# Starting eight expert units while the last routing is still being worked out

## The chip, the cores and the metric

The kernel runs on one core of a Trainium2 chip. Times are device microseconds of one execution; a profiled execution gives the trace. TensorE (PE) multiplies, VectorE (DVE) and ScalarE (ACT) work element by element, GpSimd (POOL) issues the DMAs that scatter rows to addresses read from a table, SyncE (SP) issues the others. The engines run their own instruction streams and wait for each other on semaphores.

## The reference

x has 3125 nodes of 256 values, and there are 50000 edges. Two GraphSAGE layers are followed by a mixture of experts:

```python
x = x + gnn(_layernorm(x), edge_index)              # two layers: mean over neighbours @ W_l + x @ W_r + b
x = x + moe(_layernorm(x))                          # _moe adds its tokens too: out = tokens + sum of experts
# _moe: softmax over 8 router scores, the two largest kept and scaled to sum 1
for e in range(E):
    h = jax.nn.gelu(tokens @ w1[e] + b1[e], approximate=False)
    y = h @ w2[e] + b2[e]
    out = out + combine[:, e:e + 1] * y
```

Only two experts of eight count for a node, so the kernel computes 6250 node-expert pairs.

## The kernel before

The nodes are 25 tiles of 128 (NT). The first 290 us build a matrix of edge counts and the first layer; that part is not touched. The stage in question begins at about 297 us.

**Sums.** For tile t TensorE adds 25 products (`aggregate`, L1306) into one of four PSUM buffers. VectorE reads them (`x2_and_var`), adds the residual and takes mean and variance; GpSimd raises the variance to -1/2 (`root`, L581); VectorE normalizes and writes the sum of both as the first content of `out` (`norm_and_sum`). TensorE turns and scores the tile two tiles later, between the products of `aggregate`.

**Routing.** Tiles go in 7 batches (`FIRST_OF` = 0, 4, 8, 12, 16, 20, 23). Per batch VectorE picks each node's two experts (`choose`), TensorE counts how many earlier nodes chose each expert (`prefix`), and VectorE turns that into row numbers (`place`). GpSimd then scatters each tile's normalized rows twice (`scatter`, L593, an indirect DMA of 128 rows), so that in `xs_dram` every expert has its rows one behind the other, in the order of the nodes. Behind the last batch VectorE lists the units: an expert's rows are cut into units of 256 (`PAIR`), the last of an expert filled up with padding. `tab_ri`, `tab_ei` and `tab_wi` hold a unit's first row, its expert, and, for every half of a unit, how many halves ahead of it must have been added to `out` before it may start.

**Units.** Then SP loads the rows of unit after unit (`load_rows`), TensorE turns them (`turn_rows`, L1439), multiplies by w1 (`hidden`, L1448) and by w2 (`result`, L1459); ScalarE copies and applies GELU (L1639, L1645); VectorE copies the expert's w1 (`keep_w1`, L1180), keeps each row's node and share (`keep_meta`) and adds b2 (`result`, L1175); ScalarE multiplies by the share (`weigh`, L1654). GpSimd adds the 128 rows of each half to their nodes in `out` with an indirect DMA that adds (L635). Four units of result rows have buffers (`ye`).

**Order of the additions.** Two halves may hold the same node, for two experts, and two such additions may not be in flight together. So GpSimd's stream is strictly in order, at most four additions are in flight, and each waits until as many ahead of it have landed as `tab_wi` says:

```python
pool.wait_ge(landed[q % NLAND], landed_before(n, q))
for d in range(1, NLAND):
    r = (q - d) % NLAND
    pool.wait_ge(landed[r], (before_it + (NLAND - 1 - r)) // NLAND * 16 + 32)
pool.wait_ge(S["ye_in"], n * HALVES + (q + 5))
```

The figure comes from counts per batch: for a half at place p, each expert's halves up to the end of batch b are counted as soon as the next expert's first half with nodes of that batch stands at p or ahead of it. The units run in rounds of four in a loop of 7 or 8 rounds; on these inputs there are 28 units, 56 halves and 7 rounds.

The first unit waits for the whole list, for all scatters and for all padding.

Of the kernel before, what the change touches and what calls it, by code (L numbers as in the profile page):

```python
# [5 lines left out]
F32 = mybir.dt.float32  # L6
# [8 lines left out]
P = 128  # L15
# [4 lines left out]
def build(nc, x, src, dst, w1l, w1r, b1, w2l, w2r, b2, router_w, ew1, eb1, ew2, eb2, out):  # L20
# [50 lines left out]
    FILLERS = 14  # L71
    XW = D + 8
    COEF, CHOSEN, NODE_ID = D, D + TOPK, D + 2 * TOPK
    assert NCH <= P and NCH * CHUNK == E and ALL_ROWS <= P and ALL_ROWS * ALL_COLS == E
    assert max(IN_BATCH) <= BATCH and FIRST_OF[-1] + BATCH <= NB * BATCH
    assert NW == NG * WPP and NW * WD == NT * P and NGROUP * GW == NW and NEED[-1] == NGROUP and KEYS <= P and GW == 2 * OF_BANK and OF_BANK % HALF == 0 and OF_BANK * P == 512

    with ExitStack() as ctx:
# [166 lines left out]
        end_i = later([NE], I32)  # L245
        assert oh_used[0] <= 2 * GW * (P + KEYS)

# [13 lines left out]
        def expert(shape, dt):  # L261
            n = 2
            for d in shape:
                n *= d
            if moe_used[0] % AC == 0:
                moe_used[0] += 2 * KD * D
            if moe_used[0] // AC != (moe_used[0] + n - 1) // AC:
                moe_used[0] = (moe_used[0] // AC + 1) * AC + 2 * KD * D
            assert moe_used[0] % AC + n <= AC
            return later(shape, dt, adj_flat, moe_used)  # L270
# [11 lines left out]
        hid_ps = [counts_ps[:, 2 + s, :] for s in range(2)]  # L282
# [19 lines left out]
        spread = adj[0:2 * NTAB, 2 * NE + 1, SPARE_AT - 4 * NTAB:SPARE_AT]  # L302
# [64 lines left out]
        def groups_of(t):  # L367
            return range(NEED[t + LEAD - 1], NEED[t + LEAD]) if t + LEAD < NT else range(0)

# [19 lines left out]
        def _(sp):  # L389
# [84 lines left out]
            with sp.Fori(FREE_TILES + NE, NT - 2) as t:  # L474
                node_tile(t)
            sp.wait_ge(S["zx_taken"], NT - 1)
            sp.dma_start(zi[:, :], z2_dram[(NT - 1) * P:, :]).then_inc(S["z_in"], 16)
            sp.dma_start(xt[0:LAST, :], x[(NT - 1) * P:N, :]).then_inc(S["x_in"], 16)
            sp.wait_ge(S["u_ready"], NT - 1)
            sp.dma_start(out[(NT - 2) * P:(NT - 1) * P, :], uo).then_inc(S["u_out"], 16)  # L480
            sp.wait_ge(S["u_ready"], NT)
            sp.dma_start(out[(NT - 1) * P:, :], uo[0:LAST, :]).then_inc(S["u_out"], 16)
            pad_experts(sp, range(0, NE // 2))
            for s in range(NLAND):
                sp.wait_ge(landed[s], 32)
            sp.wait_ge(S["table"], 1)

# [11 lines left out]
            load_rows(first_row, 0)  # L499
            load_rows(row_of(1), 1)  # L500
            third_row = row_of(2)
            sp.wait_ge(S["xe_tr"], 1)
            sp.wait_ge(S["meta_in"], 1)
            load_rows(third_row, 0)
            rounds = sp.value_load(nround_i[0:1, 0:1], min_val=MIN_ROUNDS, max_val=MAX_ROUNDS)

            with sp.Fori(0, rounds) as n:
# [15 lines left out]
        def _(pool):  # L523
# [59 lines left out]
            def scatter(t, j):  # L583
# [3 lines left out]
                for k in range(TOPK):  # L587
                    if t == 0:
                        g.indirect_dma_start(xs_dram, bass.IndirectOffsetOnAxis(
                            ap=slots[:, t * TOPK + k:t * TOPK + k + 1], axis=0), tok[t % KEPT], None,  # L590
                            bounds_check=NE * REGION - 1, oob_is_err=False).then_inc(scattered[t % 2], 16)
                    else:
                        g.indirect_dma_start(xs_dram, bass.IndirectOffsetOnAxis(  # L593
                            ap=slots[:, t * TOPK + k:t * TOPK + k + 1], axis=0),
                            tok[t % KEPT], None).then_inc(scattered[t % 2], 16)
# [22 lines left out]
            for t, j in to_scatter[NT - BATCH - 1:]:  # L618
                scatter(t, j)

            pool.wait_ge(S["table"], 1)
            pool.wait_ge(S["u_out"], 16 * NT)
            rounds = pool.value_load(nround_i[0:1, 0:1], min_val=MIN_ROUNDS, max_val=MAX_ROUNDS)
            with pool.Fori(0, rounds) as n:
                for q in range(HALVES):
                    u, h = q // 2, q % 2
                    before_it = pool.value_load(tab_wi[0:1, bass.ds(n * HALVES + q, 1)], min_val=0, max_val=2 * MAX_PAIRS)

                    pool.wait_ge(landed[q % NLAND], landed_before(n, q))
                    for d in range(1, NLAND):  # L630
                        r = (q - d) % NLAND
                        pool.wait_ge(landed[r], (before_it + (NLAND - 1 - r)) // NLAND * 16 + 32)
                    pool.wait_ge(S["ye_in"], n * HALVES + (q + 5))
                    pool.sem_inc(S["pool_held"], 1)
                    g.indirect_dma_start(out, bass.IndirectOffsetOnAxis(ap=ids[u][:, h:h + 1], axis=0), ye[u][:, h, :],  # L635
                                         None, bounds_check=N - 1, oob_is_err=False, compute_op=ALU.add
                                         ).then_inc(landed[q % NLAND], 16)
# [38 lines left out]
        def _(dve):  # L676
# [360 lines left out]
            def choose(j):  # L1037

                dve.wait_ge(S["logits"], FIRST_OF[j] + IN_BATCH[j])
# [9 lines left out]
                for q in range(IN_BATCH[j]):  # L1049
# [14 lines left out]
                                ).then_inc(S["masks"], 1)  # L1064
                dve.wait_ge(S["expd"], j + 1)
# [8 lines left out]
            def place(j):  # L1074

                dve.wait_ge(S["prefix"], j + 1)
                link(v.tensor_tensor(pos, bank[3][:, 0:BATCH * NE].rearrange("p (t e) -> p t e", e=NE),
                                     hist[:, j:j + 1, :].to_broadcast((P, BATCH, NE)), ALU.add))
                last = v.tensor_tensor(hist[:, j + 1, :], hist[:, j, :], bank[3][:, BATCH * NE:(BATCH + 1) * NE], ALU.add)
# [17 lines left out]
            for t in range(NT):  # L1097
                x2_and_var(t)
                j = t // BATCH
                if t % BATCH == 2 and 0 < j < NB - 1:  # L1100
                    place(j - 1)
                if t == NT - 1:
                    place(NB - 2)
                norm_and_sum(t)
                if t % BATCH == 0 and 0 < j < NB - 1:
                    choose(j - 1)
                if t == FIRST_OF[NB - 1]:
                    choose(NB - 2)

            def reached_by_batch():  # L1110
# [5 lines left out]
                link(v.tensor_copy(reached, reached_i))  # L1116
                v.tensor_tensor(weight[:, 0:NB - 1, :], reached[:, NB + 1:, 0:NE - 1], reached[:, NB:2 * NB - 1, 0:NE - 1],
                                ALU.subtract)

            reached_by_batch()  # L1120
            choose(NB - 1)
            place(NB - 1)

            link(v.tensor_tensor(nt_i, hist[:, NB, :], round_up, ALU.add))
            link(v.tensor_scalar(nt_i, nt_i, PAIR.bit_length() - 1, None, ALU.logical_shift_right))
            link(v.tensor_copy(nt, nt_i))
            link(v.tensor_tensor(summed, upto, nt.rearrange("p (a e) -> p a e", a=1).to_broadcast((P, NE, NE)), ALU.mult))
            v.scalar_tensor_tensor(weight[:, NB - 1, :], nt[:, 0:NE - 1], 2.0, reached[:, 2 * NB - 1, 0:NE - 1],
# [13 lines left out]
            for k, (lo, n) in enumerate(((0, NTAB), (NTAB, NTAB), (2 * NTAB, 2 * NTAB))):  # L1142
                last = v.tensor_scalar(spread[:, lo:lo + n], ident[0:2 * NTAB, 0:n], entry[0:2 * NTAB, k:k + 1], None, ALU.mult)
# [549 lines left out]
```

## Time and profile before

| | us |
|---|---|
| median of 3 runs (591.64 to 593.94) | 593.08 |
| the profiled execution, its own time | 592.88 |
| its span in the trace | 591.2 |
| last product of the sums begins | 443.95 |
| row numbers of the last batch written | 457.63 |
| last scatter to `xs_dram` begins | 462.42 |
| first `result` of a unit on TensorE begins | 476.15 |
| first addition to `out` begins | 480.98 |
| last addition to `out` begins | 588.09 |

In a row of the timeline stand start and length in us, engine, line, operation, tiles and shapes, a count, and in brackets how long the engine had stood idle before it and what ended that. `PE bank L1459` is line 1459 of the kernel before. Busy time of TensorE runs to modelled ends.

### The profile page before, as it was taken

The page shows a single profiled execution, that of the slowest core. Times are in us where ns is not written, and L with a number is a line of the kernel's source. Part 1 is how long each engine was busy: PE and PEld are TensorE (multiplying, and loading weights), DVE is VectorE, ACT ScalarE, POOL GpSimd, SP SyncE. Part 2 cuts the span into 40 slices and gives each one's busy share as a digit, 9 for nine tenths or more (in the row PEclk, how much of TensorE's full clock was granted, in tenths as well). Part 3 has the DMA queues.
Part 4 walks back from the last instruction along what each step waited for, and adds up shares of the span by engine and source line. Part 5 has one row for each costly group of instructions (what it writes and reads, how often), then busy time and mean ns, then how long its engine had stood idle before and what let it go on. Part 6 is the DMA issues. An engine that isn't in the chain of part 4 may idle for free.

```text
span 591.2 us, 11509 instructions
## 1 busy us (share of the span) xinstructions
PE 554.3 (94%) x3050; PEld 336.3 (57%) x3051; DVE 364.7 (62%) x1219; ACT 222.2 (38%) x422; POOL 185.5 (31%) x180
## 2 busy tenths in 40 slices
PE   4999999999999999999999999999991499999996
PEld 3555555555555555555445555555551488888885
DVE  5998667667657667663255766767678334444442
ACT  4676845434444434443101100000000155555554
POOL 3751000000000000000040154443356237787887
PEclk9999999999999999999999999999996799999999
DMA  8421211111111111012642146673332757787776
GB/s 259 148 79 60 65 45 54 48 34 54 44 37 55 37 44 54 28 55 53 196 129 80 55 137 200 202 245 126 106 130 97 228 109 118 125 142 129 129 116 92
DMA packets 64343, 61.24 MB, mean 104 GB/s; under 512 B 11281, under 2 KB 62334, under 8 KB 64302
## 3 DMA queue, kind: packets, MB, share of 16 engines
q1 hardware_dynamic: 47422, 44.84, 25.2%
q0 software_dynamic: 11200, 14.40, 13.1%
q10 hardware_dynamic: 5680, 1.49, 1.2%
q8 instruction: 21, 0.34, 0.2%
q14 instruction: 20, 0.16, 0.1%
HBM read 32.34 MB, written 29.30 MB: 104 GB/s over the span
## 4 chain that ended last, share of the span: by engine, by line
PE 69%; DMA 9%; DVE 8%; issue 8%; POOL 4%; SPq 1%; ACT 0%; POOLq 0%; DVEq 0%; ACTq 0%
PE bank L1306 22%; PE counts_ps L1448 8%; PE bank L1459 8%; PE bank L1221 8%; PE bank L1296 7%; PE counts_ps L662 7%; PE counts_ps L1306 4%; POOL xs_dram L593 2%; DMA rows<-in_x 2%; PE counts_ps L1439 2%; DMA xs_dram<-w,onehots 2%; DMA y<-y_dram 2%; PE bank L1211 1%; POOL stat L581 1%; PE bank L1289 1%
## 5 line engine op out<-in xcount | busy, mean ns | idle before, releaser
L1306 PE MATMUL bank<-y,adj 128*128 128x512 f16 x625 | 154.7, 379 | 0.4 <-ACT zt L1519 0.4
L1306 PE MATMUL counts_ps<-y,adj 128*128 128x512 f16 x625 | 144.0, 379 | 2.0 <-DMA y<-y_dram 2.0
L669 ACT ACTIVATE adj<-counts_ps 128x1000 f32 (+1 forms) x80 | 80.2, 1005 | 59.2 <-PE counts_ps L662 59.2
L635 POOL DMA_INDIRECT out<-adj x56 | 88.4, 1578 | 37.9 <-ACT adj L1654 18.5
L1306 PEld LDWEIGHTS counts_ps<-y,adj 128*128 128x128 f16 x625 | 60.7, 101 | 64.7 <-DMA y<-y_dram 4.3
L1306 PEld LDWEIGHTS bank<-y,adj 128*128 128x128 f16 x625 | 57.9, 97 | 59.5 <-issue 13.7
L565 POOL IOTA onehots<- 128x8 int32 x1 | 0.1, 143 | 225.4 <-PE counts_ps L662 225.4
L1448 PE MATMUL counts_ps<-adj 128*128 128x256 f32 x240 | 57.0, 380 | 0.0
L662 PEld LDWEIGHTS counts_ps<-onehots 125*128 125x128 f16 x640 | 42.4, 98 | 23.6 <-ACT adj L669 11.0
L648 DVE TENSOR_TENSOR onehots<-iota,lo_t 125x1024 f16<-125x1024 f16 x80 | 54.7, 684 | 1.8 <-issue 0.9
L1618 ACT ACTIVATE rows<-bank 128x256 f32<-128x256 f32 x25 | 9.6, 384 | 123.0 <-PE bank L1380 123.0
L648 DVE TENSOR_TENSOR onehots<-iota,key_t 125x1000 f16<-125x1000 f16 x80 | 53.7, 671 | 0.0
L1459 PE MATMUL bank<-adj 128*128 x224 | 53.0, 379 | 0.0
L662 PE MATMUL counts_ps<-onehots 125*128 125x125 f16 x640 | 51.0, 221 | 0.3 <-DVE onehots L648 0.3
L1221 PE MATMUL bank<-w,rows 128*128 128x512 f32 x100 | 48.8, 611 | 1.5 <-issue 1.3
L1448 PEld LDWEIGHTS counts_ps<-adj 128*128 128x128 f32 x240 | 44.9, 190 | 7.2 <-issue 1.2
L1296 PE MATMUL bank<-w,rows 128*128 128x512 f32 x100 | 47.0, 592 | 0.0
L1459 PEld LDWEIGHTS bank<-adj 128*128 128x128 f32 x224 | 40.5, 190 | 4.4
L1654 ACT ACTIVATE adj<-adj 128x256 f32<-128x256 f32 x56 | 25.4, 501 | 46.0 <-DVE adj L1175 46.0
L581 POOL TENSOR_TENSOR stat<-stat 128x1 f32<-128x1 f32 x25 | 14.2, 570 | 72.8 <-DVE stat L1019 72.8
L1175 DVE TENSOR_TENSOR adj<-bank,adj 128x512 f32<-128x512 f32 x28 | 19.4, 691 | 27.1 <-PE bank L1459 27.1
L1512 ACT ACTIVATE yo<-bank,scl_i 128x256 f16<-128x256 f32 x23 | 10.9, 475 | 58.1 <-PE bank L1296 58.1
(237 smaller groups left out, 646.6 us busy)
## 6 DMA issues: line engine op xcount, KB each, us to landing
adj<-xs_dram SPq DMA_DIRECT2D x31, 264.0 KB
rows<-z_dram SPq DMA_DIRECT2D x49, 128.0 KB, 2.1
z_dram<-zt SPq DMA_DIRECT2D x33, 128.0 KB, 1.7
adj<-in_L_ffn_w SPq DMA_DIRECT2D x16, 256.0 KB, 3.2
rows<-in_x SPq DMA_DIRECT2D x24, 128.0 KB
out<-yo SPq DMA_DIRECT2D x24, 128.0 KB
y_dram<-yo SPq DMA_DIRECT2D x23, 128.0 KB, 1.7
y<-y_dram SPq DMA_DIRECT2D x4, 640.0 KB, 6.8
```

Source lines behind the costliest of these rows:

```text
L581: g.tensor_tensor(stat[:, 8:9], stat[:, 9:10], stat[:, 10:11], ALU.pow).then_inc(S["rstd_in"], 1)
L635: g.indirect_dma_start(out, bass.IndirectOffsetOnAxis(ap=ids[u][:, h:h + 1], axis=0), ye[u][:, h, :], None, bounds_check=N - 1, oob_is_err ...
L648: last = nc.vector.tensor_tensor(oh[0:RUN, slot, :].rearrange("p (g k w) -> p g k w", k=n, w=HALF), iota_4[0:RUN, 0:n, :].rearrange("p (g ...
L662: last = nc.tensor.matmul(counts_ps[:, 2 * slot + bank_of, at * P:at * P + KEYS], stat_g[:, :, h:h + 1].rearrange("p k a -> p (k a)"), mov ...
L669: nc.scalar.activation(adj[:, :, bass.ds(at, GW * WD)].rearrange("p b (h d) -> p b h d", d=WD), counts_ps[:, 2 * (group % 2):2 * (group % ...
L1175: v.tensor_tensor(ysum[s], y_ps[s], ew(eb2_sb, e, 0).rearrange("p (h n) -> p h n", h=1) .to_broadcast((P, 2, D)), ALU.add).then_inc(S["ysu ...
L1221: last = te.matmul(out_of[t % 2][:, :], nrm_t_of[t % 2][:, k * P:(k + 1) * P], w[:, k, :], start=(k == 0), stop=(k == KD - 1))
L1296: last = te.matmul(bank[1][:, :], nrm_t[:, k * P:(k + 1) * P], w[:, k, :], start=(k == 0), stop=(k == KD - 1))
L1306: last = te.matmul(to, adj[:, b, t * P:(t + 1) * P], y[:, b, :], start=(b == 0), stop=(b == NT - 1))
L1448: last = te.matmul(hid_ps[s][:, m * PAIR:(m + 1) * PAIR], w1_of[s][:, k, m * P:(m + 1) * P], xe_t[s][:, k * PAIR:(k + 1) * PAIR], start=(k ...
L1459: last = te.matmul(y_ps[s][:, h, :], ge_t[s][:, m * PAIR + h * P:m * PAIR + (h + 1) * P], ew(ew2_sb, e, m), start=(m == 0), stop=(m == KD ...
L1654: a.activation(ye[u][:, h, :], ysum[s][:, h, :], ACT.Copy, scale=tab_c[:, bass.ds(i * 2 + h, 1)]).then_inc(S["ye_in"], 1)
```

## The change

`EARLY` = 8 units are listed when the first 16 tiles (`EARLY_BATCH` = 4 batches) have been placed: full units of 256 rows only, expert by expert in order, at most eight in all. They need no padding. VectorE counts them behind tile 18 (`count_first`) and lists them behind tile 19 (`list_first`), TensorE spreads the list in tile 21, VectorE writes the tables there and copies the first two w1 in tile 23. SP loads the first two units while the last sums run. All engines then run the eight units as straight code, and the choosing, placing and listing of the last batch stands between them. The other 20 units are listed after that, expert by expert again, and run in the loop from round 2 on. `tab_wi` is formed for both parts; a half of the second part waits for all 16 halves of the first.

GpSimd keeps one stream: the scatters of the last tiles (`AHEAD` = 0: all of them), then the 16 early halves, then the loop. The 14 `FILLERS` (products on the identity ahead of the first unit) are gone. The padding is spread between the units.

The diff's core: the constants, GpSimd's stream, then the orders of VectorE, TensorE and ScalarE.

```diff
-    FILLERS = 14
+    EARLY_ROUNDS = 2
+    EARLY = EARLY_ROUNDS * UNITS
+    EARLY_BATCH = 4
+    LIST_AT = 21
+    AHEAD = 0
...
-            for t, j in to_scatter[NT - BATCH - 1:]:
+            for t, j in to_scatter[NT - BATCH - 1:FIRST_OF[NB - 1]]:
                 scatter(t, j)
             pool.wait_ge(S["table"], 1)
+            pool.wait_ge(S["u_out"], 16 * FIRST_OF[EARLY_BATCH])
+            for q in range(AHEAD):
+                add_half(0, q, True)
+            for t, j in to_scatter[FIRST_OF[NB - 1]:]:
+                scatter(t, j)
+            for q in range(AHEAD, EARLY_ROUNDS * HALVES):
+                add_half(q // HALVES, q % HALVES, True)
+            pool.wait_ge(S["table"], 2)
             pool.wait_ge(S["u_out"], 16 * NT)
...
-            with pool.Fori(0, rounds) as n:
+            with pool.Fori(EARLY_ROUNDS, rounds) as n:
...
+                if t == LIST_AT:
+                    dve.wait_ge(S["listed"], 1)
+                    tables(bank[2], EARLY, 0, EARLY, 0)
+                if t == LIST_AT + 2:
+                    dve.wait_ge(S["ew_in"], 16 * 3 * NE)
+                    dve.wait_ge(S["table"], 1)
+                    keep_w1(0, 0)
+                    keep_w1(1, 1)
+                norm_and_sum(t)
+                if t == FIRST_OF[EARLY_BATCH] + 2:
+                    count_first()
+                if t == FIRST_OF[EARLY_BATCH] + 3:
+                    list_first()
...
+            early_unit(2)
+            reached_by_batch()
+            early_unit(3)
+            choose_experts(NB - 1)
+            early_result(0)
+            shares(NB - 1)
+            place(NB - 1)
+            early_unit(4)
+            early_result(1)
+            early_unit(5)
+            early_result(2)
+            list_rest()
...
+            turn_rows(0, 16)
+            turn_rows(1, 16)
+            hidden(0, 0)
+            pe.wait_ge(S["sums_free"], NT + 1)
+            hidden(1, 1)
+            turn_rows(0, 32)
+            turn_token(NT - 1)
...
+            early_round(0)
+            early_round(1)
+            prefix(NB - 1)
+            for i in range(2, 4):
+                early_round(i)
+            list_units(spread, bank[0], 2)
...
+            gelu(0, 0)
+            gelu(1, 1)
+            turn_rows(2, 0)
+            phase3(NT - 1)
+            powers(NB - 1)
+            for i in range(EARLY):
+                if i == 5:
+                    act.wait_ge(S["table"], 2)
+                gelu(i + 2, i % 2)
+                turn_rows(i + 3, (i + 3) % 2)
+                weigh(i, i // UNITS, i % UNITS)
+                if 1 <= i < 5:
+                    pad_experts(act, [NE // 2 + i - 1])
```

Three places show what moved. The first is TensorE behind the last product of the sums, before: `L1380` turns the last tile, `L1391` scores it, `L1398` to `L1401` are the counts of the last batch, `L1464` the list, `L1468` the fillers, `L1439` the first two units' rows.

```order
L1306 MATMUL counts_ps<-y,adj 128x512
L1380 MATMUL bank<-ident,w 128x128 x2
L1391 MATMUL bank<-onehots,rows 128x8 x2
L1398 MATMUL bank<-onehots 128x32
L1399 MATMUL bank<-onehots 128x32
L1401 MATMUL bank<-onehots 128x8
L1464 MATMUL bank<-adj,onehots 128x144
L1466 TENSOR_LOAD adj
L1466 ISA x2
L1468 MATMUL bank<-ident 128x128 x14
L1439 MATMUL counts_ps<-ident,adj 128x128 x8
```

The same place now: `L1616` turns rows of units, `L1625` is `hidden`, `L1552` turns the last tile, `L1636` is `result`, `L1563` scores the last tile.

```order
L1478 MATMUL counts_ps<-y,adj 128x512
L1616 MATMUL counts_ps<-ident,adj 128x128 x8
L1625 MATMUL counts_ps<-adj 128x256 x8
L1616 MATMUL counts_ps<-ident,adj 128x128 x4
L1552 MATMUL bank<-ident,w 128x128 x2
L1630 TENSOR_LOAD adj
L1630 ISA x2
L1636 ISA
L1636 MATMUL bank<-adj 128x256
L1636 ISA
L1636 MATMUL bank<-adj 128x256 x3
L1563 MATMUL bank<-onehots,rows 128x8 x2
```

The last tile's score stands behind the first two units' `hidden` and the first `result`; its counts stand further down, behind the second `result` and the fourth `hidden`.

The second place is VectorE in tile 23 of the sums, now: `L1099` ends the variance, `L1300` copies a w1, `L1106` and `L1111` normalize and sum, `L1278` and `L1280` keep the rows' nodes and shares, `L1125` begins the choice of batch 5.

```order
L1099 TENSOR_SCALAR stat<-stat 128x1
L1299 TENSOR_LOAD adj
L1299 ISA x2
L1300 ISA
L1300 COPY adj<-adj 128x512
L1299 TENSOR_LOAD adj
L1299 ISA x2
L1300 ISA
L1300 COPY adj<-adj 128x512
L1106 TENSOR_SCALAR onehots<-zt,stat 128x256
L1111 TENSOR_TENSOR yo<-zt,onehots 128x256
L1278 COPY adj<-adj 128x2
```

Before, the two rows with `stat` and `onehots` stood next to each other there, and the copies stood behind the list of all units.

The third place is ScalarE at the first units, now: `L1830` copies turned rows, `L1812` the last tile, `L1816` is the exponential of the last batch, `L1836` GELU.

```order
L1830 ACTIVATE adj<-counts_ps 128x512
L1812 ACTIVATE rows<-bank 128x256
L1816 ACT_TABLE_LOAD
L1816 ACTIVATE onehots<-onehots 128x32
L1833 TENSOR_LOAD adj
L1833 ISA x2
L1836 ISA
L1836 ACT_TABLE_LOAD
L1836 ACTIVATE adj<-counts_ps,onehots 128x256
```

Before, the last exponential stood ahead of the first GELU, with one table load between them; now it stands between the second and the third unit's GELU, with two.

## Rows read from the trace of the kernel before

**Rows 1.** The profile's page, its first line: the span.

```profile
span 591.2 us, 11509 instructions
```

**Rows 2.** Timeline of TensorE: the last product of the sums, the first `result`.

```profile
443.95 0.38 PE L1306 MATMUL counts_ps<-y,adj 128*128 128x512 f16 x1
...
476.15 1.89 PE L1459 MATMUL bank<-adj 128*128 x8
```

**Rows 3.** By stretch: length, each engine's busy time (instructions), granted clock, DMA share, GB/s.

```profile
444.00:450.00 6.00, 0.42 (x5) 0.11 (x3) 4.85 (x23) 0.00 (x0) 4.67 (x6) 0.91 0.25 90
450.00:455.00 5.00, 1.72 (x9) 1.22 (x9) 3.85 (x25) 0.61 (x2) 3.78 (x5) 0.50 0.28 94
480.00:500.00 20.00, 20.00 (x104) 17.37 (x103) 8.75 (x40) 11.54 (x27) 15.65 (x10) 1.00 0.69 118
```

**Rows 4.** Timeline of GpSimd: the last scatter, then the additions.

```profile
462.42 0.96 POOL L593 DMA_INDIRECT xs_dram<-w,onehots  x1 [0.31 <-issue]
480.98 1.62 POOL L635 DMA_INDIRECT out<-adj  x1 [17.60 <-ACT adj L1654]
...
505.99 1.55 POOL L635 DMA_INDIRECT out<-adj  x1 [0.31 <-DMA out<-adj]
507.94 1.55 POOL L635 DMA_INDIRECT out<-adj  x1 [0.39 <-DMA out<-adj]
510.79 1.57 POOL L635 DMA_INDIRECT out<-adj  x1 [1.30 <-issue]
513.28 1.72 POOL L635 DMA_INDIRECT out<-adj  x1 [0.92 <-issue]
...
588.09 1.55 POOL L635 DMA_INDIRECT out<-adj  x1 [0.30 <-DMA out<-adj]
```

**Rows 5.** All additions of line 635: durations, and time from issue to landing.

```profile
L635 POOL DMA_INDIRECT out<-adj x56: 1553/1555/1735, 481.0 to 588.1; - x56
...
DMA to landing us min/median/max: 2.8/3.9/4.2
```

**Rows 6.** Timeline of VectorE: two waits for sums, the last batches, the list, w1 copies.

```profile
419.35 0.48 DVE L1012 SCALAR_TENSOR_TENSOR zt<-counts_ps,rdeg,zt 128x256 f32<-128x256 f32 x1 [1.79 <-PE counts_ps L1306]
...
437.35 0.48 DVE L1012 SCALAR_TENSOR_TENSOR zt<-counts_ps,rdeg,zt 128x256 f32<-128x256 f32 x1 [0.68 <-PE counts_ps L1306]
...
443.65 0.16 DVE L1063 TENSOR_TENSOR onehots<-onehots 128x16 f16<-128x16 f16 x1
...
449.89 0.43 DVE L1031 TENSOR_TENSOR yo<-zt,w 128x256 f32<-128x256 f32 x1
...
457.63 0.17 DVE L1095 CAST onehots<-onehots 128x8 uint32<-128x8 f32 x1
457.71 0.16 DVE L1124 TENSOR_TENSOR adj<-onehots 128x8 int32<-128x8 f32 x1
...
460.75 0.14 DVE L1145 TENSOR_SCALAR adj<-adj 128x1 int32<-128x1 int32 x1
...
465.68 0.43 DVE L1180 COPY adj<-adj 128x512 f32 x1 [0.96 <-issue]
...
479.14 0.43 DVE L1180 COPY adj<-adj 128x512 f32 x1 [0.18 <-issue]
```

**Rows 7.** Timeline of ScalarE: a table load, GELU of a unit, a copy of turned rows.

```profile
462.97 1.28 ACT L1634 ACT_TABLE_LOAD   x1 [9.76 <-issue]
...
474.25 0.84 ACT L1645 ACTIVATE adj<-counts_ps,onehots 128x256 f32<-128x256 f32 x2 [1.25 <-PE counts_ps L1448]
474.98 0.60 ACT L1639 ACTIVATE adj<-counts_ps 128x512 f32<-128x512 f32 x1
```

**Rows 8.** Groups of GpSimd by line: count, busy us, mean ns, idle us before.

```profile
L593 POOL DMA_INDIRECT xs_dram<-onehots x24 | 24.0, 1001 | 10.2 <-issue 5.5 <-DVE onehots L1095 4.3 <-DMA xs_dram<-onehots 0.3
...
L589 POOL DMA_INDIRECT xs_dram<-w,onehots x2 | 2.4, 1180 | 1.9 <-DVE onehots L1095 1.6 <-issue 0.3
```

**Rows 9.** DMA issues between 425 and 470 us: KB each, us to landing.

```profile
xs_dram<-biases ACTq DMA_DIRECT2D x4, 264.0 KB, 3.0
```

More of the change, by code:

```diff
@@ L587, in scatter @@
                 for k in range(TOPK):
[L588 to L595, printed above, removed]
+                    g.indirect_dma_start(xs_dram, bass.IndirectOffsetOnAxis(
+                        ap=slots[:, t * TOPK + k:t * TOPK + k + 1], axis=0),
+                        tok[t % KEPT], None).then_inc(scattered[t % 2], 16)
                 if 0 < t <= NT - KEPT:
@@ L617, in _, with add_half @@
                     scatter(*to_scatter[t - BATCH - 1])
-            for t, j in to_scatter[NT - BATCH - 1:]:
+            def add_half(n, q, full):
+                u, h = q // 2, q % 2
+                before_it = pool.value_load(tab_wi[0:1, bass.ds(n * HALVES + q, 1)], min_val=0, max_val=2 * MAX_PAIRS)
+                pool.wait_ge(landed[q % NLAND], landed_before(n, q))
+                for d in range(1, NLAND):
+                    r = (q - d) % NLAND
+                    pool.wait_ge(landed[r], (before_it + (NLAND - 1 - r)) // NLAND * 16 + 32)
+                pool.wait_ge(S["ye_in"], n * HALVES + (q + 5))
+                pool.sem_inc(S["pool_held"], 1)
+                at = bass.IndirectOffsetOnAxis(ap=ids[u][:, h:h + 1], axis=0)
+                if full:
+                    g.indirect_dma_start(out, at, ye[u][:, h, :], None, compute_op=ALU.add).then_inc(landed[q % NLAND], 16)
+                else:
+                    g.indirect_dma_start(out, at, ye[u][:, h, :], None, bounds_check=N - 1, oob_is_err=False,
+                                         compute_op=ALU.add).then_inc(landed[q % NLAND], 16)
@@ L622, in _ @@
             pool.wait_ge(S["u_out"], 16 * NT)
             rounds = pool.value_load(nround_i[0:1, 0:1], min_val=MIN_ROUNDS, max_val=MAX_ROUNDS)
-            with pool.Fori(0, rounds) as n:
+            with pool.Fori(EARLY_ROUNDS, rounds) as n:
                 for q in range(HALVES):
[L626 to L637, printed above, removed]
+                    add_half(n, q, False)
@@ L1095, in place @@
                 v.tensor_copy(slots[:, FIRST_OF[j] * TOPK:(FIRST_OF[j] + BATCH) * TOPK], slot_f).then_inc(S["slots"], 1)
[L1097 to L1108, printed above, removed]
+            at_p = meta[:, 0:1, NODE_ID - D:NODE_ID - D + 1].rearrange("p t c -> p (t c)")
@@ new lines, in early_result @@
+            def early_result(i):
+                result(i, i // UNITS, i % UNITS)
+            for t in range(NT):
+                x2_and_var(t)
+                j = t // BATCH
+                if t % BATCH == 2 and 0 < j < NB - 1:
+                    place(j - 1)
+                if t == NT - 1:
+                    place(NB - 2)
+                if t == LIST_AT:
[11 more added lines that the diff above has]
+                    list_first()
+                if t % BATCH == 0 and 0 < j < NB - 1:
+                    choose(j - 1)
+                if t == FIRST_OF[NB - 1]:
+                    keep_meta(0, 0, 16)
+                    keep_meta(1, 1, 16)
+                    choose(NB - 2)
@@ L1191, in _ @@
+            early_result(4)
+            dve.wait_ge(S["table"], 2)
+            for i in range(EARLY, EARLY + 3):
+                early_unit(i)
+                early_result(i - 3)
+            rounds = dve.value_load(nround_i[0:1, 0:1], min_val=MIN_ROUNDS, max_val=MAX_ROUNDS)
+            with dve.Fori(EARLY_ROUNDS, rounds) as n:
                 for u in range(UNITS):
```

285 lines of the change are left out of this document (197 added, 88 removed).

## The prediction

> **What bounds the kernel now.** I read the page's first lines, then TensorE's timeline behind the sums, busy time by stretch, and the timelines of the other engines over the last 150 us. The span is 591.2 us [rows 1]; the execution took 592.88, so 1.68 us lie around it, and it stands 0.20 below the median of 593.08.
>
> The chain runs over TensorE until the last product of the sums begins at 443.95. Then come 32.2 us in which the last batch is routed, listed, scattered and padded, until the first `result` at 476.15 [rows 2]. TensorE is busy 0.42 of the first 6 of them, and its granted clock falls to 0.50 of full, 1.2 GHz [rows 3]. This hole is what the early units are to fill.
>
> Behind it two engines are nearly equal. TensorE is busy 20.00 of 20 us [rows 3]. GpSimd shows 15.65 of 20, which looks like slack and isn't: an addition takes 1.555 us [rows 5], and about 0.305 passes before the next even where nothing holds it [rows 4], so its pace is 1.86 us a half. The 56 additions began from 480.98 to 588.09 [rows 4]: 107.1 us for 55 steps, where 55 x 1.86 = 102.3 is the floor. GpSimd also ends the span, 591.2 - 588.09 = 3.1 us behind its last start. So the question is when the first addition starts, and whether its pace holds.
>
> **What sets the pace: how many may be in flight.** `tab_wi` says for each half how many ahead of it must have landed. I worked it out with the kernel's formula from the reference's own inputs. The experts get 568, 1013, 238, 1264, 432, 590, 862 and 1283 rows, hence 3, 4, 1, 5, 2, 3, 4 and 6 units, 28 in all, which the 56 additions of the trace agree with [rows 5]. Before, every half may leave at least two in flight, except halves 15 and 16 (counted from 0), where only one may be, because the small third expert holds halves 14 and 15. The trace shows just these two late: 15 starts 4.80 us behind 13 (505.99 to 510.79), 16 starts 5.34 behind 14 [rows 4]. So from a start to the start of an addition that must see it landed 4.8 us pass, about 4 of them landing [rows 5]. With two in flight (3 x 1.86 = 5.6) that is hidden.
>
> In the first 16 tiles the experts have 373, 648, 166, 817, 278, 408, 569 and 837 rows; 1, 2, 0, 3, 1 and 1 full units of the first six make up the eight. The formula then gives:
> - nothing in flight (a full drain) ahead of halves 6, 14, 16, 26 and 30;
> - one in flight, where it costs, ahead of halves 2, 13, 25 and 32.
>
> An expert cut into a small early piece and a small late piece has few halves in each, so the next expert's first half soon needs all of them. A drain costs 4.80 - 1.86 = 2.94 us, a half with one in flight 4.80 - 2 x 1.86 = 1.08. Sum: 5 x 2.94 + 4 x 1.08 = 19.0 us, against 0.99 + 0.63 = 1.6 before [rows 4]. None of it shows in the diff as more work.
>
> **When the first addition can start.** GpSimd's stream is in order, and the scatters of tiles 23 and 24 stand ahead of it. So early results wait for the row numbers of the last batch, however early they are made. Those move as follows; a short instruction of VectorE is priced by the list of before, 18 from 457.71 to 460.89 [rows 6], 0.177 each.
> - Tiles 18 to 22: `count_first` and `list_first` are 27 short ones, 4.8. VectorE waited 1.79 for the sums of tile 20 [rows 6], so 3.0 late remain.
> - Tile 23: two w1 copies now stand between variance and normalization. In straight code one took 0.96 + 0.43 [rows 6]: 2.8. Two `keep_meta` of three short ones: 1.0. Less the 0.68 that tile 23 waited itself [rows 6], VectorE is 6.1 late with the masks of batch 5, whose last instruction ended at 443.81 [rows 6]. TensorE needs them before its last product, which moves from 443.95 to about 450.0. This wait is new, and all units stand behind it.
> - The last tile is normalized and summed at 450.32 [rows 6], now 456.4. VectorE then does unit 2 (copy and meta, 1.9), `reached_by_batch` (7 short, 1.3), unit 3 (1.9): 461.5, where the choice of the last batch begins. Its scores are there by then.
> - ScalarE gets the largest scores four short ones later, 462.2, loads the exponential's table, 1.28, takes 0.2, loads GELU's again, 1.28, runs unit 2's GELU, 0.84, and copies unit 3's rows, 0.60 [rows 7]: 466.4. Only then TensorE can run unit 3's `hidden` (8 products, 1.9 as in [rows 2]), turn unit 4 and count the last batch (seven smaller ones, 0.8, an estimate): 469.1.
> - `place`, 9 short ones, 1.6: 470.7, where it was 457.80 [rows 6]. From there to the end of the last scatter passed 5.6 us (462.42 + 0.96 [rows 4]), and 0.3 to the next start: the first addition at about 477, only 4 us earlier than 480.98.
>
> The loads, turns and products of the first units lie beside this and cost nothing. The fillers' removal costs nothing if the clock stays up, as the early units are the work now; if it has fallen in the waits at 445 to 450, some 4 us (rival 4).
>
> One rule bears on the two table loads. The trace has 1.28 us for a load [rows 7]. The Trainium skill (ScalarE: Activation LUTs, What ACT_TABLE_LOAD costs) gives a load of about 1283 ns and some 1380 ns of drain with every switch. By it the two switches cost 2.8 us more, and the time is 606; the row of before began on an idle engine and can't show a drain.
>
> **The sum.** 477 + 102.3 + 19.0 + 3.1 + 1.68 = 603.1 us, 1.7% above before. Production doesn't bind: with the same prices VectorE gives results 0 to 4 at about 466, 475, 479, 486 and 490, and their additions stand at 477, 482, 485, 492 and 496.
>
> **Bounds.** The time across a wait: 4.80 and 5.34 come from a loaded stretch. The last addition, with nothing behind it, ended the span 3.1 after its start and landings go down to 2.8 [rows 5]; with the 0.6 to 0.9 between landing (3.9 to 4.2) and start that is 3.4 to 3.7. At 3.7 a drain costs 1.84 and one in flight nothing: 9.2 instead of 19.0, and 593.3. At 5.34: 5 x 3.48 + 4 x 1.62 = 23.9, and 608.0. I take 4.80, since additions and loads run right up to the drains. The first addition: 473.5 if the four w1 copies on its path cost 0.43 + 0.18 as in the loop [rows 6], 481 if the clock is down. A smaller unknown: the early additions have no bounds check. A scatter takes 1.00 without and 1.18 with one [rows 8] (two of them, one behind a pause), an addition 1.555; I take no gain, at the most 16 x 0.2 = 3.
>
> A second rule speaks for less. The trace has landings of 2.8 to 4.2 us [rows 5]. The Trainium skill (DMA: Bandwidth & Descriptors, Anatomy of one DMA — SWDGE (gpsimd) path) puts a DMA at about 2.0 us plus its bytes over 436 GB/s; for 131 KB that is 2.3, an estimate from the page, below every landing here. By it a wait takes 3.2, five drains cost 6.7, and the time is 590.8.
>
> **Rivals.**
> 1. Waits are cheap, since in a drain little else is in flight: 593. For it: the landing of 2.8. Against: the two waits of before, at 4.8 and 5.3.
> 2. TensorE binds, not GpSimd. Unit 8's rows may only be loaded when all padding has landed, and ScalarE issues the last piece behind unit 4's `weigh`, at about 492; with 3.0 to land [rows 9] and as much again to load, unit 8 is turned at 498 and its `result` comes at 506, where it was 476.15 + 8 x 3.9 = 507.4: one us gained, 592. This is the change not doing what it says: eight units early, the ninth on time. It decides only if additions don't hold; half 16 stands at 477 + 41 = 518.
> 3. Faster, by VectorE. If each value load in straight code hides behind the instruction ahead of it, as in the loop (0.18 instead of 0.96 [rows 6]), each w1 copy saves 0.8: the first addition comes at 473.5, and unit 8 up to 7 us earlier than in rival 2. From a wait of under 3.7 on the time is below 590; at 3.4 it is 473.5 + 102.3 + 7.7 + 4.8 = 588.3. Against: the slow row stands in straight code, and the price of a wait must fall too.
> 4. The clock falls in the waits at 445 to 450 and again where TensorE waits for unit 8: first addition at 481, 607. For it: 0.50 at 450 to 455 after an idle stretch [rows 3].
>
> **How the numbers follow.** Forecast 0.50, rivals 1 and 2 together 0.25, rival 3 0.12, rival 4 0.13. A measurement can tell 0.5%, 3 us, from no change. Slower than 596: the forecast, rival 4, a little of rival 1: 0.66. From 590 to 596: 0.21. Below: 0.13. The range goes from 588, which takes in rivals 1 to 3, to 612, the upper bounds together (481 + 102.3 + 23.9 + 4.8). The forecast's own range is 597 to 609.
>
> **What would show it.** GpSimd's timeline: first addition at 473 to 481, directly behind the scatters; extra gaps of about 3 us ahead of halves 6, 14, 16, 26 and 30, put down to landings of `out`; elsewhere 1.86. The last product of the sums at about 450, with TensorE waiting for VectorE before it. TensorE no longer 20 of 20 busy behind 480. I am wrong if steps across those halves stay below 3.5 us, if the first addition starts before 470, or if the additions follow TensorE's 3.9 a unit throughout.

## The result and the profile after

The changed kernel takes 605.17 us (median of 4 runs, 602.98 to 606.93) against 593.17 beside it: 1.0204 times as long, 95% interval 1.0164 to 1.0243. The prediction's sum was 603.1 with a range of 588 to 612, and slower as the likeliest outcome. The execution that was profiled took 606.93, with a span of 605.0.

GpSimd's timeline answers to [rows 4]; in brackets stand the idle time ahead of an addition and what ended it. The places of the halves (0, 1, 2, 5, 6, 13 to 16, 25, 26, 30 to 32 and 55, in this order) are counted from the first row of `out<-adj`; L696 is the straight code, L698 the loop.

```profile
472.43 0.96 POOL L658 DMA_INDIRECT xs_dram<-w,onehots  x1 [0.30 <-issue]
473.69 1.63 POOL L696 DMA_INDIRECT out<-adj  x1 [0.30 <-issue]
475.62 1.58 POOL L696 DMA_INDIRECT out<-adj  x1 [0.30 <-issue]
479.53 1.55 POOL L696 DMA_INDIRECT out<-adj  x1 [2.32 <-DMA out<-adj]
...
485.44 1.55 POOL L696 DMA_INDIRECT out<-adj  x1 [0.31 <-DMA out<-adj]
490.49 1.55 POOL L696 DMA_INDIRECT out<-adj  x1 [3.51 <-issue]
...
505.12 1.55 POOL L696 DMA_INDIRECT out<-adj  x1 [1.96 <-DMA out<-adj]
510.04 1.55 POOL L696 DMA_INDIRECT out<-adj  x1 [3.37 <-issue]
511.89 1.55 POOL L696 DMA_INDIRECT out<-adj  x1 [0.31 <-ACT adj L1845]
517.78 1.67 POOL L698 DMA_INDIRECT out<-adj  x1 [4.34 <-issue]
...
537.50 1.56 POOL L698 DMA_INDIRECT out<-adj  x1 [2.96 <-DMA out<-adj]
542.89 1.55 POOL L698 DMA_INDIRECT out<-adj  x1 [3.84 <-issue]
...
553.58 1.55 POOL L698 DMA_INDIRECT out<-adj  x1 [3.54 <-issue]
555.43 1.55 POOL L698 DMA_INDIRECT out<-adj  x1 [0.30 <-issue]
559.32 1.55 POOL L698 DMA_INDIRECT out<-adj  x1 [2.33 <-DMA out<-adj]
...
601.97 1.55 POOL L698 DMA_INDIRECT out<-adj  x1 [0.30 <-DMA out<-adj]
```

The first addition starts 7.3 us earlier than before (473.69 against 480.98), the last 13.9 later (601.97 against 588.09). Between them lie 128.3 us, where it was 107.1. The idle times of 2 to 4.3 us stand at exactly the nine halves that the formula had named, 2, 6, 13, 14, 16, 25, 26, 30 and 32; from 32 on the pace is 1.855 to the end. Ahead of the five full drains the profile says `issue`: it found nothing that ended the wait. That it was a landing is read from the formula here, and from the landings themselves in run 5.

Busy time of the engines by stretch (columns as in [rows 3]):

```profile
444.00:450.00 6.00, 4.55 (x29) 3.02 (x28) 5.31 (x33) 3.07 (x6) 3.12 (x4) 1.00 0.34 102
...
455.00:461.00 6.00, 4.79 (x27) 3.93 (x25) 3.94 (x29) 2.52 (x5) 3.85 (x5) 1.00 0.56 178
461.00:466.00 5.00, 4.24 (x16) 3.52 (x17) 1.83 (x9) 2.33 (x7) 0.00 (x0) 0.66 0.00 0
480.00:500.00 20.00, 16.10 (x76) 13.70 (x75) 7.26 (x35) 7.67 (x18) 13.82 (x10) 0.91 0.72 135
```

The hole of before is filled: TensorE is busy 4.55 of 6 us from 444 on, where it was 0.42. From 480 to 500 it is busy 16.10 of 20, where it was all 20. That drop is not the work of the waits for landings: the missing 3.90 us are one wait for the ninth unit's rows (490.12 in TensorE's timeline, shown further down), and run 1, where no addition waits for another's rows, has 16.59 there. From unit 8 on, the group of VectorE's node copies says what holds production: VectorE may write a unit's `ids` only when that buffer's additions have landed.

```profile
L1292 DVE CAST adj<-adj 128x2 uint32 (+1 forms) x28 | 5.1, 182 | 52.8 <-DMA out<-adj 48.1
```

VectorE stood 48.1 us behind additions, where it was 20.8 before. There results wait for additions, not additions for results.

### The profile page after: what moved, and what is told of

Read it like the earlier page. It is cut to its first block, busy times and chain, and to the rows that moved or that the text cites. A ratio compares the mean times of both kernels' runs of the same rounds, so it can differ in the third digit from the quotient of the medians.

```text
span 605.0 us, 11278 instructions
## 1 busy us (share of the span) xinstructions
PE 556.5 (92%) x3023; PEld 334.0 (55%) x3024; DVE 368.5 (61%) x1256; ACT 223.7 (37%) x424; POOL 184.7 (31%) x180
## 4 chain that ended last, share of the span: by engine, by line
PE 53%; DMA 15%; issue 13%; DVE 8%; POOL 5%; POOLq 3%; ACT 1%; ACTq 1%; DVEq 0%; SPq 0%
PE bank L1478 22%; DMA out<-adj 9%; PE bank L1393 8%; PE counts_ps L742 7%; PE bank L1468 7%; PE counts_ps L1478 4%; POOL xs_dram L658 3%; DMA rows<-in_x 2%; POOLq L686 2%; DMA y<-y_dram 2%; PE counts_ps L1625 1%; POOL stat L651 1%; POOLq L691 1%; PE bank L1383 1%; DMA xs_dram<-w,onehots 1%
## 5 line engine op out<-in xcount | busy, mean ns | idle before, releaser
L1625 PE MATMUL counts_ps<-adj 128*128 128x256 f32 x240 | 60.3, 397 | 18.2 <-ACT adj L1830 17.2
L698 POOL DMA_INDIRECT out<-adj x40 | 62.3, 1558 | 27.8 <-issue 13.9
L1625 PEld LDWEIGHTS counts_ps<-adj 128*128 128x128 f32 x240 | 46.2, 196 | 28.3 <-issue 20.8
L1636 PE MATMUL bank<-adj 128*128 x224 | 54.4, 386 | 2.3 <-ACT adj L1836 1.9
L1812 ACT ACTIVATE rows<-bank 128x256 f32<-128x256 f32 x25 | 9.6, 382 | 113.7 <-PE bank L1552 113.7
L1468 PE MATMUL bank<-w,rows 128*128 128x512 f32 x100 | 47.0, 592 | 0.0
L1636 PEld LDWEIGHTS bank<-adj 128*128 128x128 f32 x224 | 41.1, 193 | 7.8 <-issue 3.0
L1292 DVE CAST adj<-adj 128x2 uint32 (+1 forms) x28 | 5.1, 182 | 52.8 <-DMA out<-adj 48.1
```

Source lines behind the costliest of these rows:

```text
L698: g.indirect_dma_start(out, at, ye[u][:, h, :], None, bounds_check=N - 1, oob_is_err=False, compute_op=ALU.add).then_inc(landed[q % NLAND] ...
L1468: last = te.matmul(bank[1][:, :], nrm_t[:, k * P:(k + 1) * P], w[:, k, :], start=(k == 0), stop=(k == KD - 1))
L1625: last = te.matmul(hid_ps[s][:, m * PAIR:(m + 1) * PAIR], w1_of[s][:, k, m * P:(m + 1) * P], xe_t[s][:, k * PAIR:(k + 1) * PAIR], start=(k ...
L1636: last = te.matmul(y_ps[s][:, h, :], ge_t[s][:, m * PAIR + h * P:m * PAIR + (h + 1) * P], ew(ew2_sb, e, m), start=(m == 0), stop=(m == KD ...
```

## The experiments

Theory A: the waits for landings, which the new order of the units makes, cost the time; without them the change gains. Rivals: B, production (all that makes a unit's result rows) is late, since the work moved ahead slows VectorE, ScalarE or TensorE, and the waits only show it; C, the chip's clock or the loaded DMA queues slow all additions alike.

**1. No waits for landings, in the changed kernel.** The additions go to rows of their own for each expert, so no two halves can hold the same row and `tab_wi` is 0 everywhere; at most four stay in flight. The instructions of GpSimd are the same.

```diff
-                    g.indirect_dma_start(out, at, ye[u][:, h, :], None, compute_op=ALU.add)
+                    g.indirect_dma_start(apart_dram, at, ye[u][:, h, :], None, compute_op=ALU.add)
...
-                v.tensor_copy(ids[u], tab_id[:, bass.ds(i * 2, 2)])
+                v.tensor_scalar(ids[u], tab_id[:, bass.ds(i * 2, 2)], tab_off[:, bass.ds(i, 1)], float(NE), ALU.add, ALU.mult)
...
-                v.tensor_scalar(tab_wi[:, 2 * lo:2 * hi], of[:, 2 * n + 2 * lo:2 * n + 2 * hi], float(halves_too), None, ALU.add
+                v.tensor_scalar(tab_off[:, lo:hi], of[:, n + lo:n + hi], float(NE - 1), 1.0 / NE, ALU.min, ALU.mult)
+                v.tensor_scalar(tab_wi[:, 2 * lo:2 * hi], of[:, 2 * n + 2 * lo:2 * n + 2 * hi], 0.0, None, ALU.mult
```

> The changed kernel with the additions going to rows that no other expert shares (row = 8 x node + expert of a scratch tensor), so that no addition has to wait for another's rows; four in flight stay. It leaves the experts' results out of the output. Theory A (the order of the additions on GpSimd costs the time): first addition still at 474, steps of 1.86 across halves 6, 14, 16, 26 and 30, last one at 576 to 580, 581 to 586 us in all. Theory B (the early units are made too late, TensorE and its clock set the end): steps stay long because rows aren't there, 600 us or more.

Measured: 583.75 us (582.55 to 585.91), ratio to before 0.9856, interval 0.9821 to 0.9892. Halves 0, 11, 12 and 55 in GpSimd's timeline:

```profile
471.16 1.63 POOL L699 DMA_INDIRECT apart_dram<-adj  x1 [0.30 <-issue]
...
492.02 1.55 POOL L699 DMA_INDIRECT apart_dram<-adj  x1 [0.30 <-DMA apart_dram<-adj]
496.70 1.55 POOL L699 DMA_INDIRECT apart_dram<-adj  x1 [3.13 <-ACT adj L1849]
...
578.92 1.55 POOL L701 DMA_INDIRECT apart_dram<-adj  x1 [0.30 <-DMA apart_dram<-adj]
```

The 55 steps take 107.8 us instead of 128.3, 20.5 less; by the ratios (0.9856 against 1.0204) the kernel is 20.6 us shorter than the changed one. Theory A stands, and B and C fall as the main cause: the same work ahead of it, the same engines, the same number and size of additions. The largest step left is at half 12, 4.68 us behind 11 and released by ScalarE's weighing; that is production, and run 6 meets the like. Halves 16 and 32, at the heads of the loop's rounds, still take 2.86 and 2.55 us, so what they have over the pace in the changed kernel is not all the waits'.

**2. The same edit in the kernel before**, for comparison: if writing elsewhere were itself cheaper, this would be faster too.

> The same separate rows in the kernel before, which also leaves the experts' results out of the output. Theory A: only halves 15 and 16 waited there, 1.6 us, and TensorE's 3.9 us a unit is next: 590 to 593 us. Theory B says the same. If separate rows made additions themselves cheaper, this run would show it: under 588.

Measured: 593.76 us (592.05 to 595.40), ratio 1.0007 (0.9987 to 1.0026). Writing elsewhere gives nothing, and the waits of before gave away no more than can be measured. So the difference in run 1 comes from the waits of the changed order.

**3. Two additions ahead of the scatters.**

```diff
-    AHEAD = 0
+    AHEAD = 2
```

> The changed kernel with AHEAD = 2: the two halves of unit 0 are added ahead of the scatters of the last two tiles, in the 8.4 us in which GpSimd waits for their row numbers. Theory A: additions 0 and 1 near 463 and 465, half 2 at about 474 instead of 479.5 without a wait, everything behind it 5.8 earlier: 599 us. Theory B: the units behind aren't ready earlier, 604 to 606.

Measured: 600.70 us (599.81 to 601.87), ratio 1.0136 (1.0105 to 1.0166): by the ratios 4.0 us less than the changed kernel, where 5.8 had been expected. GpSimd's timeline, halves 0 and 2; half 1 (at 465.75) and the scatters lie between them:

```profile
463.82 1.62 POOL L696 DMA_INDIRECT out<-adj  x1 [2.97 <-issue]
...
474.28 1.61 POOL L696 DMA_INDIRECT out<-adj  x1 [0.30 <-issue]
```

Halves 0 and 1 run while GpSimd would wait for the row numbers, and the wait ahead of half 2 lies beside the scatters: half 2 starts at 474.28 instead of 479.53. That confirms a part of the prediction, that the scatters in GpSimd's order hold the first additions. It also shows that the first start alone does not decide: 9.9 us earlier gave 4.0, and the kernel is still slower than before.

**4. Fewer cuts.** The eight early units come from experts 3, 6 and 7 only (3, 2 and 3 units) instead of from experts 0, 1, 3, 4 and 5. By the formula two full drains are left, ahead of halves 16 and 32. Two added instructions of VectorE, nothing else:

```diff
+                link(v.scalar_tensor_tensor(full, iota_e, 2.0, full, ALU.is_ge, ALU.mult))
+                link(v.scalar_tensor_tensor(full, full, 2.0, full, ALU.is_ge, ALU.mult))
```

> The changed kernel with other early units: on these inputs the full units of experts 3, 6 and 7 (3, 2 and 3) in place of 1, 2, 3, 1 and 1 of experts 0, 1, 3, 4 and 5; as many early units, and the work on every other engine the same. By the wait formula full drains fall from five to two (halves 16 and 32). Theory A: at 5.1 us across a wait the 55 steps take 111 us instead of 124 (128 measured): 589 to 593 us. Theory B: no change, 603 to 606.

Measured: 593.48 us (591.17 to 596.49), ratio 1.0005 (0.9983 to 1.0028), just above the 589 to 593 that were expected. As much early work, the same places in all streams, and by the ratios 11.8 us gone. The two drains are where the formula has them, as the addition ahead of each and the delayed one show (halves 15, 16, 31 and 32):

```profile
504.07 1.55 POOL L696 DMA_INDIRECT out<-adj  x1 [0.31 <-DMA out<-adj]
509.88 1.55 POOL L698 DMA_INDIRECT out<-adj  x1 [4.26 <-issue]
...
540.10 1.55 POOL L698 DMA_INDIRECT out<-adj  x1 [2.44 <-DMA out<-adj]
545.73 1.75 POOL L698 DMA_INDIRECT out<-adj  x1 [4.09 <-issue]
```

The 55 steps took 117.5 us, not the 111 expected. Besides the drains, halves 7 and 31, which by the formula may leave only one in flight, took 3.18 and 3.99 us, and half 12, for which it asks no such wait, took 3.62.

**5. The price of a drain by itself**, in the kernel before, whose front and units are untouched:

```diff
+                    if q == 6:
+                        before_it = n * HALVES + q
```

> The kernel before, with one edit: half 6 of every round waits until all halves ahead of it have landed (7 full drains in 56 additions). If a full drain has a price of its own, about 3.2 us as in the changed kernel's trace (5 drains, 17.0 us over the pace), and isn't a matter of that kernel's front or of what else runs there: 7 x 3.2 = 22.4, less some 1 us of the one-in-flight wait ahead of half 15 that the drain ahead of 14 takes in: 593.2 + 21.4 = 614.6 (611 to 618). If a drain is cheap where production isn't late (rival: the changed kernel pays for late results, not for the waits): at most 600.

Measured: 618.55 us (616.22 to 619.47) against 594.75, ratio 1.0390 (1.0354 to 1.0427). The first two of the seven drains, each behind the addition ahead of it:

```profile
492.23 1.55 POOL L637 DMA_INDIRECT out<-adj  x1 [0.30 <-DMA out<-adj]
496.16 1.55 POOL L637 DMA_INDIRECT out<-adj  x1 [2.37 <-issue]
...
509.92 1.55 POOL L637 DMA_INDIRECT out<-adj  x1 [0.30 <-DMA out<-adj]
515.20 1.64 POOL L637 DMA_INDIRECT out<-adj  x1 [3.72 <-issue]
```

The seven steps are 3.93, 5.28, 5.20, 5.12, 4.93, 5.66 and 5.04 us, 5.02 in the mean: 3.16 over the pace, close to the 3.2 that was expected. The trace also has when the addition ahead of each drain landed (line 637, in a window around that addition alone): 2.7, 4.1, 4.0, 3.8, 3.7, 4.4 and 3.8 us after its start. The next one started 1.2 to 1.3 us after the landing every time, so a drain is one landing and 1.2 us. The whole costs 23.8 us (618.55 - 594.75), somewhat over the 21.4 expected. A drain leaves a little behind, too: the second halves after the first six, which stand at the heads of the loop's rounds (8, 16, 24, 32, 40 and 48), take 16.6 us together, where they took 13.8 in the kernel before. So a drain costs about 3.2 to 3.4 us in the mean, in either kernel.

**6. Both edits, 3 and 4, together.**

> Changed kernel with both edits: the eight early units come from three experts only (3, 6 and 7: 3, 2 and 3 units) so that two full drains are left instead of five, and two early additions start ahead of the scatters of the last two tiles. The two gains should add, since the one shortens the stretch of additions and the other moves work in front of it: 593.5 - 4.5 = 589.0 (586 to 592), 0.7% faster than before. Rival: production binds as soon as the waits are short, then 592 to 594, the same as without the early additions.

Measured: 594.62 us (592.67 to 597.51), ratio 0.9995 (0.9976 to 1.0014). The gains did not add; the rival named there, production, fits. GpSimd's timeline shows it at half 10, which starts 5.22 us behind half 9 and has idled 3.67:

```profile
494.11 1.55 POOL L696 DMA_INDIRECT out<-adj  x1 [3.67 <-ACT adj L1847]
```

It waits for ScalarE's weighing, and that for VectorE, whose timeline names the reason:

```profile
490.86 0.17 DVE L1280 COPY adj<-adj 128x2 f32<-128x2 f32 x1 [6.83 <-DMA adj<-xs_dram]
```

The ninth unit's rows come at 490.86, because they may be read only when all padding has landed. VectorE takes their nodes (L1280) ahead of the result of unit 5 (L1297), so that result stands behind rows that it has nothing to do with. This is the mechanism of rival 2 of the prediction, at another place than it had named. Run 7 tries it.

**7. The padding earlier**, otherwise as run 6:

```diff
-                if 1 <= i < 5:
-                    pad_experts(act, [NE // 2 + i - 1])
+                if 1 <= i < 3:
+                    pad_experts(act, [NE // 2 + 2 * i - 2, NE // 2 + 2 * i - 1])
```

> The changed kernel with three early experts, two additions ahead and one more edit: ScalarE issues its four pieces of padding behind the weighing of units 1 and 2, two each, instead of one each behind units 1 to 4. In the run without this edit the ninth unit's rows arrived at 490.86, VectorE waited 6.83 us for them with the result of unit 5 queued behind, and addition 10 started 3.4 us late. If that wait is what ate the gain (production binds through the last padding): rows 6 us earlier, addition 10 at the pace, 594.6 - 3.4 = 591.2 (589 to 593). If the time follows the full drains alone, 594 to 595 as before the edit.

Measured: 590.29 us (588.48 to 591.59) against 593.73, ratio 0.9946 (0.9925 to 0.9967). By the ratios that is 2.9 us less than run 6, 3.4 had been expected, and it is the fastest complete version here: 0.54% faster than the kernel before, interval 0.33 to 0.75. The ninth unit's rows come 7.0 us earlier than in run 6:

```profile
483.88 0.20 DVE L1280 COPY adj<-adj 128x2 f32<-128x2 f32 x1 [1.36 <-DMA adj<-xs_dram]
```

The busy time by stretch of run 6 and, below it, of this run:

```profile
480.00:490.00 10.00, 6.40 (x32) 5.31 (x30) 2.75 (x14) 3.86 (x9) 7.14 (x5) 1.00 0.80 144
490.00:500.00 10.00, 9.12 (x38) 7.58 (x39) 4.58 (x23) 3.62 (x8) 4.02 (x4) 0.83 0.71 134
```

```profile
480.00:490.00 10.00, 9.88 (x52) 8.53 (x51) 5.19 (x26) 5.54 (x13) 7.57 (x5) 1.00 0.87 154
490.00:500.00 10.00, 10.00 (x52) 8.82 (x51) 3.88 (x18) 5.52 (x14) 7.78 (x6) 1.00 0.80 142
```

TensorE no longer waits for rows at 486 to 491 (9.88 of 10 instead of 6.40), and the clock no longer falls behind it (1.00 instead of 0.83). Half 10 is at the pace; apart from half 2 behind the scatters, the largest steps left are the drains ahead of 16 and 32, of 5.36 and 5.79 us. The two profiled executions took 596.23 and 588.48 us, further apart than the medians, so these rows show more than the 2.9 us.

**8. The same padding without the two additions ahead** (run 4 with the edit of run 7).

> The same edit on the padding with three early experts, but no addition ahead of the scatters. There the additions waited about 1.3 us ahead of half 7 and 1.8 ahead of half 12. If those came from late results through the ninth unit's rows: 593.5 - 1.8 = 591.7 (590 to 593.5); if from landings alone, 593.5 as without the edit.

Measured: 592.17 us (591.37 to 593.96), ratio 0.9976 (0.9963 to 0.9990): by the ratios 1.7 us less than run 4, but the intervals of the two ratios overlap. Of the two late halves half 12 is back at the pace, as expected of late results; half 7 isn't (3.82 us), and by the formula it has a wait of its own. The two additions ahead are worth 1.9 us here (590.29 on the same chip), where they were worth nothing in run 6; these intervals touch, too, so both steps are likely, not shown.

## Why the prediction was right, point by point

**The waits.** This step carried the forecast, and the trace has it at the nine halves named, in the kind named. Its size was too small. From the start of an addition to the start of one that must see it landed, 4.80 us was taken. The five full drains took 5.05, 4.92, 5.89, 5.39 and 5.09 us, which is 17.0 over the pace of 1.86, where 14.7 was predicted. The four halves with one in flight took 3.91, 3.50, 4.72 and 3.89: 8.6 over the pace, where 4.3 was predicted. Together 25.6 instead of 19.0. This is the mis-sized term: counted from the addition two places ahead, which they wait for, those four took 5.84, 5.36, 6.62 and 5.74 us, longer than 4.80 and longer than most full drains. The prediction drew one duration from two rows, made it of a landing of 3.9 to 4.2 and 0.6 to 0.9 until the next start, and used it for both kinds. In the changed kernel the traced landings that such halves waited for, those of halves 0, 11 and 23, came after 4.8, 4.4 and 5.5 us, and the start 1.0 to 1.2 later; in run 5 it was 1.2 to 1.3.

Not all of the 25.6 is the waits': without any (run 1) halves 16 and 32 were still 1.00 and 0.69 over the pace. The prediction had also misread the trace of before, where halves 15 and 16 are not "just these two late": half 8 came 2.40 us behind 7 and half 32 came 3.12 behind 31, with no wait for landings named by the formula.

```profile
544.89 1.55 POOL L635 DMA_INDIRECT out<-adj  x1 [1.39 <-issue]
```

So 25.6 is an upper figure. Leaving the waits out (run 1) gave 20.5, with half 12 then late by production.

The Trainium skill (DMA: Bandwidth & Descriptors, Anatomy of one DMA — SWDGE (gpsimd) path) makes a landing of about 2.3 us from 2.0 plus the bytes over the rate, an estimate from that page. The trace does not agree: landings of the additions to `out` have 2.7, 3.9 and 5.6 us as least, middle and most in the changed kernel (28 of the 56 are in the trace).

**The first addition.** It came at 473.69, not 477. Along the steps of the prediction, in us:

| step | predicted | trace |
|---|---|---|
| last product of the sums | 450.0 | 446.98 |
| last tile's sum done | 456.4 | 452.84 |
| choice of the last batch begins | 461.5 | 457.42 |
| unit 3's rows copied by ScalarE | 466.4 | 461.62 |
| last batch counted | 469.1 | 465.90 |
| row numbers of the last batch | 470.7 | 467.58 |
| first addition | 477 | 473.69 |

The order of the steps held, and from the row numbers on the lengths too (6.1 against 6.3). The loss of 3 us was at the first step, VectorE in tile 23 (timeline of VectorE, answering to [rows 6]; sum read, variance, two w1 copies, normalization, last mask):

```profile
438.74 0.48 DVE L1092 SCALAR_TENSOR_TENSOR zt<-counts_ps,rdeg,zt 128x256 f32<-128x256 f32 x1
...
440.57 0.15 DVE L1099 TENSOR_SCALAR stat<-stat 128x1 f32<-128x1 f32 x1
441.42 0.43 DVE L1300 COPY adj<-adj 128x512 f32 x1 [0.69 <-issue]
442.19 0.43 DVE L1300 COPY adj<-adj 128x512 f32 x1 [0.34 <-issue]
442.53 0.41 DVE L1106 TENSOR_SCALAR onehots<-zt,stat 128x256 f32<-128x256 f32 x1
...
446.67 0.16 DVE L1148 TENSOR_TENSOR onehots<-onehots 128x16 f16<-128x16 f16 x1
```

Tile 23 began 1.39 late (438.74 against 437.35), not 2.3. From variance to normalization passed 1.96 us. In the kernel before the same stretch held a wait of 0.76 for GpSimd, whose rows in VectorE's timeline are these:

```profile
439.19 0.15 DVE L1019 TENSOR_SCALAR stat<-stat 128x1 f32<-128x1 f32 x1
440.11 0.41 DVE L1026 TENSOR_SCALAR onehots<-zt,stat 128x256 f32<-128x256 f32 x1 [0.76 <-POOL stat L581]
```

So the two copies added 1.96 - 0.92 = 1.04 us, not 2.8: the idle time ahead of them, in which their registers are loaded, was 0.69 and 0.34 instead of 0.96, and they filled a wait that the prediction had not looked for. The two `keep_meta` took 0.70 instead of 1.0. VectorE was 3.0 late, not 6.1.

Behind that, two errors cancelled. On ScalarE (answering to [rows 7]) the exponential's table cost nothing, since its load stands ahead of the wait for the scores:

```profile
454.01 1.28 ACT L1816 ACT_TABLE_LOAD   x1
458.24 0.23 ACT L1816 ACTIVATE onehots<-onehots 128x32 f32<-128x32 f32 x1 [2.95 <-DVE onehots L1132]
458.99 1.28 ACT L1836 ACT_TABLE_LOAD   x1 [0.52 <-issue]
460.29 0.84 ACT L1836 ACTIVATE adj<-counts_ps,onehots 128x256 f32<-128x256 f32 x2
```

The GELU begins 0.02 us behind its load. The Trainium skill (ScalarE: Activation LUTs, What ACT_TABLE_LOAD costs) gives some 1380 ns of drain with a switch; between the exponential's end at 458.47 and the load lie 0.52 us here, so the trace agrees with its 1283 ns for the load and not with a drain of that size. Against this gain stands TensorE's clock, in its timeline (answering to [rows 2]):

```profile
446.98 0.38 PE L1478 MATMUL counts_ps<-y,adj 128*128 128x512 f16 x1
...
461.76 3.29 PE L1625 MATMUL counts_ps<-adj 128*128 128x256 f32 x8 [1.97 <-ACT adj L1830]
...
468.64 1.99 PE L1625 MATMUL counts_ps<-adj 128*128 128x256 f32 x8 [0.91 <-DVE adj L1300]
...
490.12 1.12 PE L1616 MATMUL counts_ps<-ident,adj 128*128 128x128 f32 x4 [3.90 <-DMA adj<-xs_dram]
491.03 2.90 PE L1636 MATMUL bank<-adj 128*128 x8
```

Unit 3's `hidden` took 3.29 us at a granted clock of 0.66 over 461 to 466, between the levels of 1.2 and 2.4 GHz; the next took 1.99 at full clock. The counts of the last batch stand behind it.

**The sum.** 473.69 + 102.3 + 25.6 + 0.4 elsewhere + 3.0 + 1.93 = 606.9, the profiled execution. Against the forecast, -3.3 at the front and +6.6 in the waits: that the time came out within 2.1 us of the median is in part luck, by errors of opposite sign; the direction isn't.

**The rivals.** 1, cheap waits: false, by runs 1, 4 and 5. 2, TensorE bound by the ninth unit's rows: TensorE did wait 3.90 us for them, but that unit's `result` came at 499.82, not 506, and its first addition only at 517.78. It decided nothing here, and decided in run 6. The prediction's sign that TensorE would no longer be busy for 20 of 20 us behind 480 came true by this wait, not by the waits that it was to show. 3, cheap w1 copies: its first half came out, 473.5 for the first addition, in part by cheaper copies and in part by the wait that they filled; its second, cheap waits, didn't. 4, the clock: it didn't fall in the waits at 445 to 450 (granted 1.00); it fell behind the wait of 1.97 us at 460, and, as this rival had said, again where TensorE waited for unit 8 (granted 0.85 from 490 to 500, a `result` of 2.90 us instead of 1.89). The first addition came at 473.69 all the same, not 481. The bounds check, left out of the early additions, changes nothing: 16 without it have 1547, 1549 and 1668 ns as least, middle and most, 40 with it 1547, 1549 and 1746.

## What to carry to other kernels

Before work is moved ahead, work out what its order does to the waits behind it: here a table of counts, evaluated on the real inputs, named all nine places, and no line of the diff did. An engine that looks 78% busy can be at its pace; take starts, not busy times, and price a wait from start to start in the kind that it is (nothing in flight, or one). When a bound is lifted, read which wait comes next before adding the gains: on top of the fewer cuts, the early additions were worth nothing until the padding had moved too.

## What the hardware showed that was not expected

- In the changed kernel an addition that must see the last but one landed, with one in between under way, started 5.36 to 6.62 us behind it; with nothing behind it, the landing was seen after 4.92 to 5.89. The one in between doesn't explain it by itself: from 564 on, where additions follow one another at the pace, landings took 2.7 to 4.3 us. What made the landings of halves 0 and 23 longer (4.8 and 5.5) stays open.
- The first six w1 copies in straight code had 0.69, 0.34, 0.32, 0.90, 0.57 and 0 us of idle time of their engine ahead of them; in the loop of before it was mostly 0.17 or 0.18.
- After a busy stretch of TensorE (4.79 of 6 us, granted 1.00) one wait of 1.97 us was followed by a granted clock of 0.66, between the levels of 1.2 and 2.4 GHz. What sets the moment of the fall stays open.
